# v projected with the tokens on the partitions, and placed by 16 DMAs a strip

## The chip, the core and the metric

The kernel runs on one core of one Trainium2 chip. Its time is the device time of one execution in microseconds (us). Engines: TensorE (PE in the profile), VectorE (DVE), ScalarE (ACT), GpSimd (POOL), SyncE (SP); PEld is the loading of weights, which overlaps PE. The data are float32 but for the gates.

## The reference

x is (8, 64, 96, 96). Two passes of window attention (4x4 windows, 8 heads of 4 channels, for each half of the channels) are made on the normalized x, the second on rows rolled by two; then a mixture of experts per pixel. Cut to what matters:

```python
qkv = einsum('oi,bihw->bohw', qkv_w, xh)            # xh: 32 channels of layernorm(x)
q, k, v = split(qkv, 3, axis=1)
lepe = depthwise_conv3x3(v, lepe_w)
attn = softmax(einsum('nhqc,nhkc->nhqk', q*scale, k) + bias)   # n: window, 16 tokens
out = einsum('nhqk,nhkc->nhqc', attn, v) + lepe
x = x + pass(shift 0) + pass(shift 2)
t = tokens(x); y = layernorm(t)
t = t + sum over the top 2 of 8 experts of gate * (y @ expert_w[e] + expert_b[e])
```

## The kernel before

The image is worked in strips of 4 rows (384 pixels, 24 windows): 24 strips an image, 192 in all. On the partitions lie 4 groups of 32 channels: both halves of the channels of both passes, so one strip serves both. A strip is three units of 8 windows. The whole program is a software pipeline of slots, one unit a slot, three a strip, six a tile (two strips of the experts' part). Every engine walks the same slots in order, and in each slot does the stages whose turn it is; `LAG` gives for each stage how many slots it comes after a strip's (or unit's) first. There is no scheduler: an engine's instructions run in program order, and semaphores join the engines. A stage of strip k at lag L stands in slot 3k+L; a stage that is done for each unit stands in slots 3k+L to 3k+L+2.

The stages around the change:

- `centre` (lag 0) and `variance` (1): TensorE centres the strip, ScalarE makes the reciprocal deviation, and VectorE multiplies (L989), which signals `xn_made`.
- `value` (2): TensorE multiplies the strip by `wv` (L570, for attention) and `wo` (L572, for the convolution); ScalarE evicts the first twice, once for each value of a mask, into `v2` (L697), and the second into the padded image `vpad` (L701).
- `query_key` (3), `spread_k` (4): q and k; GpSimd spreads k by 4 DMAs (L476).
- `turn_v` (5): VectorE transposes `v2` to `v2t` in 32x32 blocks (L939).
- `tap_products` (6), `pool_taps` (7), `taps` (10): nine taps of the convolution. ScalarE makes three products, one a slot (L744); GpSimd adds the second and third to the first (L493), in the slots 3k+8 and 3k+9; VectorE does the other six, two a slot (L906), and the first of them waits for both of GpSimd's additions (L902). ScalarE's second and third product of a strip wait for GpSimd's addition of the strip before (L742).
- `spread_v` (7): GpSimd places `v2t` into `vx`, the weights of the product, by 4 DMAs (L484). It waits for `v2t_made`, and, `vx` having two buffers, for the products of strip k-2 (L481).
- `score` (7), `shift` (8), `turn_p` (10), `product` (11): scores by 32x32 tiles (L541), softmax without its division, transposed probabilities (L981), 32 small matmuls with `vx` as weights (L607), and in a strip's last unit the sums over `ones` (L612); then `pv_made` rises by one.
- `experts` (35): TensorE spreads a gate (L516), VectorE multiplies (L895), TensorE applies the expert (L525), eight times a tile; before the change the first expert of a slot comes ahead of `value`.

```python
wait_alone(pool, v2t_made, k + 1)
if s.later(r, 2):
    wait_alone(pool, pv_made, (k - 1) * UNITS)
```

Of the kernel before, what the change touches and what calls it, by code (L numbers as in the profile page):

```python
# [32 lines left out]
ALU = mybir.AluOpType  # L33
# [6 lines left out]
SP = 4  # L40
# [26 lines left out]
    spread_k=4, turn_v=5, place_bias=6, spread_v=7, score=7, shift=8,  # L67
# [80 lines left out]
def _constants():  # L148
    p = np.arange(128)
    g, c = p // CH, p % CH  # L150
    same64 = (p[:, None] // C == p[None, :] // C).astype(np.float32)
    parts = {
        "ident": np.eye(128),
        "centre": np.eye(128) - same64 / C,
        "mean": same64 / C,

        "mask_q": ((p[:, None] // 16 & 1) == np.arange(2)[None, :]) * HD ** -0.5,
        "mask_v": (p[:, None] & 1) == np.arange(2)[None, :],
        "ones": (p[:, None] // 32 == np.arange(32)[None, :] // 8) & (p[:, None] // TOK % 2 == np.arange(32)[None, :] % 2),
        "mask_b": (p[:, None] // TOK % 4) == p[None, :4],  # L160

        "expert_sel": np.stack([(p[:, None] % E == e) & (p[:, None] // E % 2 == p[None, :] // C)
                                & (p[:, None] < 3 * GE) for e in range(E)], axis=1).reshape(128, E * 128),
        "rank": np.tile(E - np.arange(E), (128, 1)),
        "eps1": np.full((128, 1), LN1_EPS),
        "eps2": np.full((128, 1), LN2_EPS),
    }
# [10 lines left out]
def metaformer_block(nc, x, qkv_w, lepe_w, bias_table, router_w, router_b, expert_w, expert_b, consts, out):  # L178
    ctx = ExitStack()
    with ctx:  # L180
# [43 lines left out]
        v2 = sb("v2", [128, 2, WIN, 2, TOK])  # L224
        v2t = sb("v2t", [128, 2, 8, WIN, 4])
        qx = sb("qx", [128, 2, WIN, 2, TOK])
        kx = sb("kx", [128, 2, 4, SPX])
        vx = sb("vx", [128, 2, 32, WIN * 4])
# [38 lines left out]
        v2_made, v2t_made = sem("v2_made"), sem("v2t_made")  # L267
# [49 lines left out]
        X_DMAS, Z_DMAS, TILE_DMAS, K_DMAS, V_DMAS = 5, 11, 7, 4, 4  # L317
# [4 lines left out]
        def _(sp):  # L322
# [134 lines left out]
        def _(pool):  # L457
# [7 lines left out]
            G.memset(vx[:, :, :, :].rearrange("p a c n -> p (a c n)"), 0.0).then_inc(spread_cleared, 1)  # L465
# [3 lines left out]
            def slot(s):  # L469
# [29 lines left out]
        def _(pe):  # L499
# [9 lines left out]
            def slot(s):  # L509
# [20 lines left out]
                if u := s.unit("score"):  # L530
# [34 lines left out]
                if st := s.strip("value"):  # L565
                    k, r = st
                    pe.wait_ge(xn_made, k + 1)
                    if ti := s.tile("router"):
                        pe.wait_ge(fln_made, ti[0] + 1)
                    MM(bank_p[0][:, 0:SPX], wv[:, :], xs[:, r % 4, :], start=True, stop=True).then_inc(v_made, 1)  # L570
                    pe.wait_ge(ln_made, k + 1)
                    MM(bank_p[1][:, 0:SPX], wo[:, :], xs[:, r % 4, :], start=True, stop=True).then_inc(vo_made, 1)  # L572
                if st := s.strip("query_key"):
# [4 lines left out]
                    MM(bank_p[1][:, 0:SPX], wk[:, :], xs[:, r % 4, :], start=True, stop=True).then_inc(k_made, 1)  # L578
                if st := s.strip("query_key"):
                    k, r = st  # L580
                    pe.wait_ge(v2_made, (k + 1) * 2)
                    MM(bank_p[0][:, 0:SPX], wq[:, :], xs[:, r % 4, :], start=True, stop=True).then_inc(q_made, 1)  # L582
# [10 lines left out]
                if u := s.unit("product"):  # L593
# [10 lines left out]
                    for w in range(UW):  # L604
                        at = (j * UW + w)
                        for c in range(4):
                            last = MM(bank_o[32 * c:32 * c + 32, at * TOK:(at + 1) * TOK],  # L607
                                      vx[:, kr % 2, :, at * 4 + c],
# [45 lines left out]
        def _(act):  # L654
# [12 lines left out]
            def slot(s):  # L667
# [23 lines left out]
                if st := s.strip("value"):  # L691
                    k, r = st
                    act.wait_ge(v_made, k + 1)
                    if s.later(r, 2):
                        act.wait_ge(v2t_made, k - 1)
                    for x in range(2):
                        S.activation(v2[:, r % 2, :, x, :].rearrange("p n (r w) -> p n r w", w=SP),  # L697
                                     windows(bank_p[0][:, 0:SPX]), ACT.Copy,
                                     scale=const("mask_v")[:, x:x + 1]).then_inc(v2_made, 1)
                    act.wait_ge(vo_made, k + 1)  # L700
                    S.activation(vrows(r, 0, 0), bank_p[1][:, 0:SPX].rearrange("p (r w) -> p r w", w=W),  # L701
# [12 lines left out]
                if st := s.strip("query_key"):  # L714
# [4 lines left out]
                    for a in range(2):  # L719
                        S.activation(qx[:, r % 2, :, a, :].rearrange("p n (r w) -> p n r w", w=SP),  # L720
                                     windows(bank_p[0][:, 0:SPX]), ACT.Copy,
                                     scale=const("mask_q")[:, a:a + 1]).then_inc(q_saved, 1)
                if st := s.strip("query_key"):
# [5 lines left out]
                    S.activation(by_window(k_sb[:, r % 2, :]), windows(bank_p[1][:, 0:SPX]),  # L729
# [35 lines left out]
        def _(dve):  # L765
# [13 lines left out]
            for g in range(4):  # L779
# [3 lines left out]
                for b in range(2):  # L783
                    some = heads_of(2, g).rearrange("p (h a b y) -> p b h a y", h=HD, a=2, b=2)[:, b]
                    V.tensor_copy(wv[:, g * CH + 16 * b:g * CH + 16 * b + 16].rearrange("p (a h y) -> p h a y", a=2, y=2), some)
# [89 lines left out]
            def slot(s):  # L875
# [58 lines left out]
                if st := s.strip("turn_v"):  # L934
                    k, r = st
                    dve.wait_ge(v2_made, (k + 1) * 2)
                    if s.later(r, 2):
                        dve.wait_ge(v_spread[r % 2], k // 2 * (V_DMAS * 16))
                    V.transpose(v2t[:, r % 2, :, :, :].rearrange("p q n k -> p n k q"), v2[:, r % 2, :, :, :].rearrange("p n x i -> p (n x i)")).then_inc(v2t_made, 1)  # L939
# [76 lines left out]
```

## Time and profile before

| | |
|---|---|
| median of 3 runs | 4068.01 us (4063.95 to 4075.65) |
| profiled execution | 4055.97 us, span 4054.1 us |
| mean granted TensorE clock | 0.967 of full speed |
| PE, DVE, ACT, POOL busy | 92%, 79%, 57%, 30% of the span |
| chain that ended last | PE 72%, DVE 12%, issue 7%, ACT 7% |
| DMA engines busy (mean of 16) | about 25% of the span |

The span is from the first to the last instruction. A busy share says how long an engine was at work, not whether anyone waited for it; the chain follows back from the last instruction to what released each step, so it says where time would be won or lost. A wait is put down to the instruction that ended it. DMAs issued by GpSimd take time on GpSimd for each of them, and that time counts as its busy time.

### The profile page before, as it was taken

What the parts mean: (1) busy time and instruction counts of PE and PEld (TensorE: products, weight loads), DVE (VectorE), ACT (ScalarE), POOL (GpSimd) and SP (SyncE); (2) the same over time, 40 slices, a digit from 0 to 9 for tenths busy, and PEclk for the clock granted to TensorE, in tenths of its full rate; (3) what the DMA queues carried; (4) which work ended last, traced back from release to release, by engine and by line L of the source; (5) the groups of instructions that cost most, each with busy time, mean ns of one, the idle gap of its engine ahead of it and who ended that gap; (6) DMA issues with size and microseconds to landing.
All of it is one profiled execution on the core that took longest, in us unless ns stands there. A gap on an engine that the chain in (4) does not pass through costs nothing.

```text
span 4054.1 us, 199188 instructions
## 1 busy us (share of the span) xinstructions
PE 3712.7 (92%) x81317; PEld 2244.7 (55%) x81317; DVE 3193.6 (79%) x7043; ACT 2299.6 (57%) x4708; POOL 1207.9 (30%) x1930
## 2 busy tenths in 40 slices
PE   3999999998999989999999989999899999999987
PEld 2655555555555555555555555555555555555552
DVE  3888888887887878787788878788788888888773
ACT  3755665655665555655555555556565656566540
POOL 2433333322333323333232323333233333333320
PEclk9999999999999999999999999999999999999985
DMA  2222222222222222222222222222222222222220
GB/s 41 79 66 75 70 76 68 78 69 68 70 74 69 74 65 75 68 75 68 68 71 68 72 66 73 68 75 69 73 69 73 70 75 67 75 69 76 67 56 22
DMA packets 191590, 278.78 MB, mean 69 GB/s; under 512 B 67584, under 2 KB 153648, under 8 KB 190640
## 3 DMA queue, kind: packets, MB, share of 16 engines
q1 hardware_dynamic: 141488, 152.22, 14.0%
q0 software_dynamic: 49152, 113.34, 9.8%
q8 instruction: 663, 10.86, 1.1%
q14 instruction: 287, 2.35, 0.2%
HBM read 95.46 MB, written 56.62 MB: 38 GB/s over the span
## 4 chain that ended last, share of the span: by engine, by line
PE 72%; DVE 12%; issue 7%; ACT 7%; SPq 1%; DVEq 1%; DMA 0%; ACTq 0%
PE bank L607 20%; PE bank L525 13%; PE bank L541 10%; DVE v2t L939 5%; PE bank L578 4%; PE bank L564 4%; PE bank L620 4%; PE bank L516 3%; PE bank L612 3%; PE bank L582 3%; DVE gx L895 3%; ACT row_inv L679 2%; PE bank L634 2%; ACT row_inv L677 2%; PE bank L639 1%
## 5 line engine op out<-in xcount | busy, mean ns | idle before, releaser
L607 PEld LDWEIGHTS bank<-probT,vx 128*32 128x32 f32 x36864 | 831.3, 193 | 201.8 <-issue 171.4
L607 PE MATMUL bank<-probT,vx 128*32 128x16 f32 x36864 | 888.4, 236 | 3.0 <-issue 2.2
L525 PE MATMUL bank<-gx,expert_sb 128*128 128x384 f32 x1536 | 714.0, 548 | 190.8 <-DVE gx L895 190.8
L895 DVE TENSOR_TENSOR gx<-bank,yn 128x384 f32<-128x384 f32 x768 | 423.6, 552 | 557.0 <-PE bank L516 554.9
L476 POOL DMA_DIRECT2D kx<-k_sb x768 | 411.3, 538 | 1194.9 <-ACT k_sb L729 1108.3
L541 PEld LDWEIGHTS bank<-kx,qx 32*32 32x32 f32 x36864 | 565.6, 108 | 302.5 <-issue 299.7
L541 PE MATMUL bank<-kx,qx 32*32 32x64 f32 x36864 | 664.3, 221 | 40.9 <-issue 31.6
L484 POOL DMA_DIRECT2D vx<-v2t x768 | 380.7, 503 | 911.0 <-PE bank L612 857.8
L493 POOL TENSOR_TENSOR lepe_p<-lepe_p,tap_sb 128x384 f32<-128x384 f32 x384 | 406.4, 1058 | 604.7 <-ACT tap_sb L744 601.2
L906 DVE SCALAR_TENSOR_TENSOR lepe<-vpad,lepe_sb,lepe 128x384 f32<-128x384 f32 x960 | 582.1, 606 | 0.0
L706 ACT ACTIVATE prob<-prob 128x512 f32<-128x512 f32 x576 | 363.1, 630 | 230.1 <-DVE prob L926 229.9
L525 PEld LDWEIGHTS bank<-gx,expert_sb 128*128 128x128 f32 x1536 | 243.5, 194 | 416.4 <-DVE gx L895 356.3
L981 DVE STREAM_TRANSPOSE probT<-prob 128x512 f32<-128x512 f32 x576 | 404.1, 702 | 0.0
L926 DVE TENSOR_TENSOR prob<-bank,row_max 128x512 f32<-128x512 f32 x576 | 393.1, 682 | 11.9 <-issue 7.8
L914 DVE TENSOR_REDUCE row_max<-bank 128x32 f32<-128x512 f32 x576 | 393.2, 683 | 11.7 <-issue 9.5
L697 ACT ACTIVATE v<-bank,const_sb 128x384 f32<-128x384 f32 x384 | 201.8, 577 | 334.2 <-PE bank L570 334.2
L720 ACT ACTIVATE qx<-bank,const_sb 128x384 f32<-128x384 f32 x384 | 205.3, 587 | 316.1 <-PE bank L582 316.1
L712 ACT ACTIVATE bank<-bias_tile 128x512 f32<-128x512 f32 x576 | 341.8, 593 | 0.0
L939 DVE STREAM_TRANSPOSE v2t<-v 128x768 f32<-128x768 f32 x192 | 291.7, 1519 | 0.2
L516 PEld LDWEIGHTS bank<-gateT,expert_sel 48*128 48x128 bf16 x768 | 71.6, 93 | 389.0 <-issue 382.6
L516 PE MATMUL bank<-gateT,expert_sel 48*128 48x384 bf16 x768 | 260.0, 338 | 0.0
L734 ACT ACTIVATE xs<-bank 128x384 f32<-128x384 f32 x192 | 94.1, 490 | 264.1 <-PE bank L620 264.1
(100 smaller groups left out, 4701.3 us busy)
## 6 DMA issues: line engine op xcount, KB each, us to landing
vx<-v2t POOLq DMA_DIRECT2D x768, 96.0 KB, 2.7
kx<-k_sb POOLq DMA_DIRECT2D x768, 48.0 KB
z<-fin SPq DMA_DIRECT2D x1344, 24.0 KB
xs<-in_x SPq DMA_DIRECT2D x96, 192.0 KB
xt<-in_x SPq DMA_DIRECT2D x192, 96.0 KB
z0t<-z SPq DMA_DIRECT2D x192, 96.0 KB
out_y<-y_out SPq DMA_DIRECT2D x192, 96.0 KB, 2.7
xs<-in_x SPq DMA_DIRECT2D x96, 139.5 KB
```

The costliest lines, as they stand in the source:

```text
L476: pool.dma_start(kx[m:128:4, r % 2, m, :], k_sb[m:128:4, r % 2, :]).then_inc(k_spread[r % 2], 16)
L493: G.tensor_tensor(lepe_p[:, kr % 2, :], lepe_p[:, kr % 2, :], tap_sb[:, j - 1, :], ALU.add).then_inc(pool_lepe_made, 1)
L516: MM(bank_g[:, 0:SPX], expert_sel[:, e, :], gateT[:, r % 2, :], start=True, stop=True)\
L525: MM(bank_f[:, 0:SPX], expert_sb[:, e, :], gx[:, e % 2, :], start=False, stop=(e == E - 1))\
L541: last = MM(bank_s[r % 2][at, w * KEYS:(w + 1) * KEYS], qx[at, kr % 2, win, :, :].rearrange("p a i -> p (a i)"), kx[at, kr % 2, :, win * T ...
L607: last = MM(bank_o[32 * c:32 * c + 32, at * TOK:(at + 1) * TOK], vx[:, kr % 2, :, at * 4 + c], probT[:, kr % 2, at, c * TOK:(c + 1) * TOK] ...
L895: V.tensor_tensor(gx[:, e % 2, :], bank_g[:, 0:SPX], yn[:, r % 2, :], ALU.mult).then_inc(gx_made, 1)
L906: V.scalar_tensor_tensor(acc, vrows(r, t // 3 - 1, t % 3 - 1), lepe_sb[:, t:t + 1], first if j == 0 else acc, ALU.mult, ALU.add).then_inc( ...
L914: V.tensor_reduce(row_max[:, r % 2, :], per_row(bank_s[r % 2][:, :]), AX.X, ALU.max).then_inc(max_made, 1)
L926: V.tensor_tensor(per_row(prob[:, r % 4, :]), per_row(bank_s[r % 2][:, :]), over_keys(row_max[:, r % 2, :]), ALU.subtract).then_inc(shifte ...
L939: V.transpose(v2t[:, r % 2, :, :, :].rearrange("p q n k -> p n k q"), v2[:, r % 2, :, :, :].rearrange("p n x i -> p (n x i)")).then_inc(v2 ...
L981: V.transpose(probT[:, kr % 2, j * UW:(j + 1) * UW, :].rearrange("p n k -> p (n k)"), prob[:, r % 4, :]).then_inc(probT_made, 1)
```

## The change

v for the attention is made with the tokens, not the channels, on the partitions. VectorE's multiply writes the normalized strip into a new buffer `xw` in the order of windows, and all four projections read it. Each pair of windows has 32 tokens; for each pair and each group of 32 channels one matmul with the 32x32 block of `xw` as weights and the block of `wv` as moving data gives 32 tokens by 32 channels, 48 matmuls a strip. ScalarE evicts them once, into `vt`. VectorE's transpose and `turn_v` are gone. GpSimd places `vt` into `vx` by 16 DMAs of 16 partitions in place of 4 of 32, as a token of an odd window has to move to another partition. `spread_v` has lag 5 in place of 7. The value matmuls stand right behind the scores, ahead of the first expert. The eviction of v waits for the DMAs of strip k-2, and the loads of x wait for `xn_made` in place of `q_made`.

```diff
-    spread_k=4, turn_v=5, place_bias=6, spread_v=7, score=7, shift=8,
+    spread_k=4, place_bias=6, spread_v=5, score=7, shift=8,
...
-        X_DMAS, Z_DMAS, TILE_DMAS, K_DMAS, V_DMAS = 5, 11, 7, 4, 4
+        X_DMAS, Z_DMAS, TILE_DMAS, K_DMAS, V_DMAS = 5, 11, 7, 4, 16
...
-                        wait_alone(sp, q_made, (k - 1) * 2)
+                        wait_alone(sp, xn_made, (k - 1) * 2)
...
                 if st := s.strip("spread_v"):
                     k, r = st
-                    wait_alone(pool, v2t_made, k + 1)
+                    wait_alone(pool, vt_saved, k + 1)
                     if s.later(r, 2):
                         wait_alone(pool, pv_made, (k - 1) * UNITS)
                     for g in range(4):
-                        rows = slice(32 * g, 32 * g + 32)
-                        pool.dma_start(vx[rows, r % 2, g * 8:g * 8 + 8, :].rearrange("p q n -> p (q n)"),
-                                     v2t[rows, r % 2, :, :, :].rearrange("p q n k -> p (q n k)")).then_inc(v_spread[r % 2], 16)
+                        for x in range(2):
+                            for odd in range(2):
+                                to, at = g * CH + x * TOK, g * CH + odd * TOK
+                                pool.dma_start(vx[to:to + TOK, r % 2, g * 8 + x:g * 8 + 8:2, odd, :],
+                                               vt[at:at + TOK, r % 2, x::2, :, :].rearrange("p h n k -> p h (n k)"))\
+                                    .then_inc(v_spread[r % 2], 16)
...
+                if st := s.strip("value"):
+                    k, r = st
+                    if ti := s.tile("router"):
+                        pe.wait_ge(fln_made, ti[0] + 1)
+                    wait_alone(pe, xn_made, k + 1)
+                    for pair in range(WIN // 2):
+                        cols = slice(pair * CH, pair * CH + CH)
+                        for g in range(4):
+                            at = slice(g * CH, g * CH + CH)
+                            last = MM(bank_p[0][at, cols], xw[at, r % 2, cols], wv[at, at], start=True, stop=True)
+                    last.then_inc(v_made, 1)
...
-                    MM(bank_p[0][:, 0:SPX], wv[:, :], xs[:, r % 4, :], start=True, stop=True).then_inc(v_made, 1)
                     pe.wait_ge(ln_made, k + 1)
-                    MM(bank_p[1][:, 0:SPX], wo[:, :], xs[:, r % 4, :], start=True, stop=True).then_inc(vo_made, 1)
+                    MM(bank_p[1][:, 0:SPX], wo[:, :], xw[:, r % 2, :], start=True, stop=True).then_inc(vo_made, 1)
...
                     if s.later(r, 2):
-                        act.wait_ge(v2t_made, k - 1)
-                    for x in range(2):
-                        S.activation(v2[:, r % 2, :, x, :].rearrange("p n (r w) -> p n r w", w=SP),
-                                     windows(bank_p[0][:, 0:SPX]), ACT.Copy,
-                                     scale=const("mask_v")[:, x:x + 1]).then_inc(v2_made, 1)
+                        act.wait_ge(v_spread[r % 2], k // 2 * (V_DMAS * 16))
+                    S.activation(vt[:, r % 2, :, :, :].rearrange("p q n k -> p n q k"),
+                                 bank_p[0][:, 0:SPX].rearrange("p (n q k) -> p n q k", q=8, k=4),
+                                 ACT.Copy).then_inc(vt_saved, 1)
...
-                    V.transpose(v2t[:, r % 2, :, :, :].rearrange("p q n k -> p n k q"), v2[:, r % 2, :, :, :].rearrange("p n x i -> p (n x i)")).then_inc(v2t_made, 1)
...
-                    V.tensor_tensor(xs[:, r % 4, :], xs[:, r % 4, :], rstd[:, r % 2, :], ALU.mult).then_inc(xn_made, 1)
+                    if s.later(r, 2):
+                        dve.wait_ge(q_made, k - 1)
+                    V.tensor_tensor(by_window(xw[:, r % 2, :]), windows(xs[:, r % 4, :]), windows(rstd[:, r % 2, :]),
+                                    ALU.mult).then_inc(xn_made, 1)
```

GpSimd's queue at the start of the pipeline, before: k's DMAs go into `kx`, v's into `vx`, and the additions on `lepe_p` are those of the convolution, two a strip.

```order
L476 DMA kx<-k_sb 32x384 [waits k_saved,const_loaded,spread_cleared]
L476 DMA kx<-k_sb 32x384 x3
L476 DMA kx<-k_sb 32x384 [waits k_saved]
L476 DMA kx<-k_sb 32x384 x3
L484 DMA vx<-v2t 32x768 [waits v2t_made]
L484 DMA vx<-v2t 32x768 x3
L493 ISA
L493 TENSOR_TENSOR lepe_p<-lepe_p,tap_sb 128x384 [waits tap_made]
L493 TENSOR_TENSOR lepe_p<-lepe_p,tap_sb 128x384 [waits pool_lepe_made,tap_made]
```

The same place after the change:

```order
L475 DMA kx<-k_sb 32x384 [waits k_saved,const_loaded,spread_cleared]
L475 DMA kx<-k_sb 32x384 x3
L485 DMA vx<-vt 16x4x48 [waits vt_saved]
L485 DMA vx<-vt 16x4x48 x15
L475 DMA kx<-k_sb 32x384 [waits k_saved]
L475 DMA kx<-k_sb 32x384 x3
L485 DMA vx<-vt 16x4x48 [waits vt_saved]
L485 DMA vx<-vt 16x4x48 x15
L495 ISA
L495 TENSOR_TENSOR lepe_p<-lepe_p,tap_sb 128x384 [waits tap_made]
L495 TENSOR_TENSOR lepe_p<-lepe_p,tap_sb 128x384 [waits pool_lepe_made,tap_made]
```

Before, v of strip 0 stands ahead of strip 0's additions; after, v of strips 0 and 1 does, and so on: v of strip k comes right ahead of the additions of strip k-1. From the third strip on v's first DMA also waits for `pv_made`, in both.

TensorE from one strip's last product to the next strip's first, before, where no experts are at work yet:

```order
L612 MATMUL bank<-probT,const_sb 32x384 x4
L541 MATMUL bank<-kx,qx 32x64 [waits bias_placed]
L541 MATMUL bank<-kx,qx 32x64 x31
L570 MATMUL bank<-xs,wv 128x384 [waits xn_made]
L572 MATMUL bank<-xs,wo 128x384 [waits ln_made]
L607 MATMUL bank<-probT,vx 32x16 [waits picked,log_made,v_spread1,probT_made]
L607 MATMUL bank<-probT,vx 32x16 x31
```

And after the change:

```order
L621 MATMUL bank<-probT,const_sb 32x384 x4
L543 MATMUL bank<-kx,qx 32x64 [waits bias_placed]
L543 MATMUL bank<-kx,qx 32x64 x31
L557 MATMUL bank<-wv,xw 32x32 [waits xn_made]
L557 MATMUL bank<-wv,xw 32x32 x47
L581 MATMUL bank<-xw,wo 128x384 [waits ln_made]
L616 MATMUL bank<-probT,vx 32x16 [waits picked,log_made,v_spread1,probT_made]
L616 MATMUL bank<-probT,vx 32x16 x31
```

One matmul over the whole strip is now 48 small ones, with the same wait ahead of them.

## Rows read from the trace of the kernel before

**Rows 1.** The page: busy us (share) and instructions, and the chain that ended last.
```profile
PE 3712.7 (92%) x81317; PEld 2244.7 (55%) x81317; DVE 3193.6 (79%) x7043; ACT 2299.6 (57%) x4708; POOL 1207.9 (30%) x1930
...
PE 72%; DVE 12%; issue 7%; ACT 7%; SPq 1%; DVEq 1%; DMA 0%; ACTq 0%
PE bank L607 20%; PE bank L525 13%; PE bank L541 10%; DVE v2t L939 5%; PE bank L578 4%; PE bank L564 4%; PE bank L620 4%; PE bank L516 3%; PE bank L612 3%; PE bank L582 3%; DVE gx L895 3%; ACT row_inv L679 2%; PE bank L634 2%; ACT row_inv L677 2%; PE bank L639 1%
```

**Rows 2.** Groups of instructions: count | busy us, mean ns | idle before, releasers.
```profile
L476 POOL DMA_DIRECT2D kx<-k_sb x768 | 411.3, 538 | 1194.9 <-ACT k_sb L729 1108.3 <-issue 59.1 <-PE bank L541 27.4
...
L484 POOL DMA_DIRECT2D vx<-v2t x768 | 380.7, 503 | 911.0 <-PE bank L612 857.8 <-issue 52.2
L939 DVE STREAM_TRANSPOSE v2t<-v 128x768 f32<-128x768 f32 x192 | 291.7, 1519 | 0.2
...
L966 DVE TENSOR_TENSOR fin<-att,lepe 128x384 f32<-128x384 f32 x192 | 105.6, 550 | 0.0
```

**Rows 3.** Line 484 alone: ns min/median/max, first and last start in us.
```profile
L484 POOL DMA_DIRECT2D vx<-v2t x768: 496/504/513, 70.8 to 3915.5; - x192
...
DMA to landing us min/median/max: 2.1/2.7/6.9
```

**Rows 4.** Waits of GpSimd: us in total, times, longest.
```profile
POOL vx L484 <- PE bank L612: 857.8, 183, 11.9
```

**Rows 5.** Timeline from 2000 us, TensorE and GpSimd: start, us, instruction [idle before].
```profile
2000.99 0.86 PE L612 MATMUL bank<-probT,const_sb 128*32 128x384 f32 x7
...
2002.50 1.98 POOL L484 DMA_DIRECT2D vx<-v2t  x4 [3.67 <-PE bank L612]
...
2003.38 1.10 PE L541 MATMUL bank<-kx,qx 32*32 32x64 f32 x64
...
2004.41 0.91 PE L525 MATMUL bank<-gx,expert_sb 128*128 128x384 f32 x2
...
2005.52 0.91 PE L570 MATMUL bank<-xs,wv 128*128 128x384 f32 x2
...
2006.26 0.81 PE L572 MATMUL bank<-xs,wo 128*128 128x384 f32 x2
...
2015.69 1.48 PE L607 MATMUL bank<-probT,vx 128*32 128x16 f32 x64
```

**Rows 6.** The same stretch, VectorE.
```profile
2001.50 0.68 DVE L914 TENSOR_REDUCE row_max<-bank 128x32 f32<-128x512 f32 x1
...
2003.58 0.56 DVE L895 TENSOR_TENSOR gx<-bank,yn 128x384 f32<-128x384 f32 x1 [1.40 <-PE bank L516]
...
2020.66 0.61 DVE L906 SCALAR_TENSOR_TENSOR lepe<-vpad,lepe_sb,lepe_p 128x384 f32<-128x384 f32 x1
...
2022.53 0.55 DVE L989 TENSOR_TENSOR xs<-xs,rstd 128x384 f32<-128x384 f32 x1
```

**Rows 7.** Timeline from 3894 us, all engines.
```profile
3896.48 0.84 PE L612 MATMUL bank<-probT,const_sb 128*32 128x384 f32 x7
...
3898.28 0.91 PE L525 MATMUL bank<-gx,expert_sb 128*128 128x384 f32 x2
...
3899.96 2.15 POOL L493 TENSOR_TENSOR lepe_p<-lepe_p,tap_sb 128x384 f32<-128x384 f32 x2
...
3902.70 1.65 PE L525 MATMUL bank<-gx,expert_sb 128*128 128x384 f32 x2 [3.24 <-DVE gx L895]
...
3904.28 1.53 PE L607 MATMUL bank<-probT,vx 128*32 128x16 f32 x64
```

**Rows 8.** Timeline of TensorE alone, a little later.
```profile
3905.74 1.93 PE L541 MATMUL bank<-kx,qx 32*32 32x64 f32 x64
```

**Rows 9.** Windows: length, busy (instructions) of PE, PEld, DVE, ACT, POOL, clock, DMA share, GB/s.
```profile
88.00:92.00 4.00, 3.52 (x67) 2.63 (x68) 3.96 (x6) 1.10 (x3) 1.00 (x1) 0.60 0.02 6
92.00:96.00 4.00, 3.70 (x132) 2.79 (x131) 3.55 (x7) 3.80 (x8) 1.13 (x1) 0.97 0.02 4
...
3960.00:3965.00 5.00, 3.70 (x6) 1.20 (x6) 2.34 (x9) 0.00 (x0) 0.00 (x0) 0.50 0.20 51
```

More of the change, by code:

```diff
@@ L157, in _constants @@
         "mask_q": ((p[:, None] // 16 & 1) == np.arange(2)[None, :]) * HD ** -0.5,
-        "mask_v": (p[:, None] & 1) == np.arange(2)[None, :],
         "ones": (p[:, None] // 32 == np.arange(32)[None, :] // 8) & (p[:, None] // TOK % 2 == np.arange(32)[None, :] % 2),
@@ L223, in metaformer_block @@
         k_sb = sb("k_sb", [128, 2, SPX])
-        v2 = sb("v2", [128, 2, WIN, 2, TOK])
-        v2t = sb("v2t", [128, 2, 8, WIN, 4])
+        xw = sb("xw", [128, 2, SPX])
+        vt = sb("vt", [128, 2, 8, WIN // 2, 4])
         qx = sb("qx", [128, 2, WIN, 2, TOK])
         kx = sb("kx", [128, 2, 4, SPX])
-        vx = sb("vx", [128, 2, 32, WIN * 4])
+        vx = sb("vx", [128, 2, 32, 2, WIN // 2 * 4])
         prob = sb("prob", [128, 4, UK])
@@ L266, in metaformer_block @@
         q_made, k_made, q_saved, k_saved = sem("q_made"), sem("k_made"), sem("q_saved"), sem("k_saved")
-        v2_made, v2t_made = sem("v2_made"), sem("v2t_made")
+        vt_saved = sem("vt_saved")
         k_spread, v_spread, spread_cleared = sems("k_spread"), sems("v_spread"), sem("spread_cleared")
@@ L464, in _ @@
             G.memset(kx[:, :, :, :].rearrange("p a c n -> p (a c n)"), 0.0).then_inc(spread_cleared, 1)
-            G.memset(vx[:, :, :, :].rearrange("p a c n -> p (a c n)"), 0.0).then_inc(spread_cleared, 1)
+            G.memset(vx[:, :, :, :, :].rearrange("p a c b n -> p (a c b n)"), 0.0).then_inc(spread_cleared, 1)
             pool.wait_ge(const_loaded, 16 * N_WEIGHT_DMAS)
@@ L566, in slot @@
                     k, r = st
-                    pe.wait_ge(xn_made, k + 1)
-                    if ti := s.tile("router"):
-                        pe.wait_ge(fln_made, ti[0] + 1)
-                    MM(bank_p[0][:, 0:SPX], wv[:, :], xs[:, r % 4, :], start=True, stop=True).then_inc(v_made, 1)
                     pe.wait_ge(ln_made, k + 1)
-                    MM(bank_p[1][:, 0:SPX], wo[:, :], xs[:, r % 4, :], start=True, stop=True).then_inc(vo_made, 1)
+                    MM(bank_p[1][:, 0:SPX], wo[:, :], xw[:, r % 2, :], start=True, stop=True).then_inc(vo_made, 1)
                 if st := s.strip("query_key"):
@@ L577, in slot @@
                     pe.wait_ge(v_saved, k + 1)
-                    MM(bank_p[1][:, 0:SPX], wk[:, :], xs[:, r % 4, :], start=True, stop=True).then_inc(k_made, 1)
+                    MM(bank_p[1][:, 0:SPX], wk[:, :], xw[:, r % 2, :], start=True, stop=True).then_inc(k_made, 1)
                 if st := s.strip("query_key"):
                     k, r = st
-                    pe.wait_ge(v2_made, (k + 1) * 2)
-                    MM(bank_p[0][:, 0:SPX], wq[:, :], xs[:, r % 4, :], start=True, stop=True).then_inc(q_made, 1)
+                    pe.wait_ge(vt_saved, k + 1)
+                    MM(bank_p[0][:, 0:SPX], wq[:, :], xw[:, r % 2, :], start=True, stop=True).then_inc(q_made, 1)
                 expert(1)
@@ L607, in slot @@
                             last = MM(bank_o[32 * c:32 * c + 32, at * TOK:(at + 1) * TOK],
-                                      vx[:, kr % 2, :, at * 4 + c],
+                                      vx[:, kr % 2, :, at % 2, at // 2 * 4 + c],
                                       probT[:, kr % 2, at, c * TOK:(c + 1) * TOK], start=True, stop=True)
@@ L719, in slot @@
                     for a in range(2):
-                        S.activation(qx[:, r % 2, :, a, :].rearrange("p n (r w) -> p n r w", w=SP),
-                                     windows(bank_p[0][:, 0:SPX]), ACT.Copy,
+                        S.activation(qx[:, r % 2, :, a, :], bank_p[0][:, 0:SPX].rearrange("p (n i) -> p n i", i=TOK), ACT.Copy,
                                      scale=const("mask_q")[:, a:a + 1]).then_inc(q_saved, 1)
@@ L728, in slot @@
                         act.wait_ge(k_spread[r % 2], k // 2 * (K_DMAS * 16))
-                    S.activation(by_window(k_sb[:, r % 2, :]), windows(bank_p[1][:, 0:SPX]),
+                    S.activation(k_sb[:, r % 2, :], bank_p[1][:, 0:SPX],
                                  ACT.Copy).then_inc(k_saved, 1)
@@ L784, in _ @@
                     some = heads_of(2, g).rearrange("p (h a b y) -> p b h a y", h=HD, a=2, b=2)[:, b]
-                    V.tensor_copy(wv[:, g * CH + 16 * b:g * CH + 16 * b + 16].rearrange("p (a h y) -> p h a y", a=2, y=2), some)
+                    V.tensor_copy(wv[:, g * CH:(g + 1) * CH].rearrange("p (h y b a) -> p b h a y", h=HD, y=2, b=2)[:, b], some)
                     last = V.tensor_copy(wo[:, 64 * b:64 * b + 64].rearrange("p (a g h y) -> p g h a y", a=2, g=4, y=2)[:, g], some)
@@ L933, in slot @@
                 gate_work((0, 0), (0, 0), (13, 14))
[L934 to L938, printed above, removed]
-                    V.transpose(v2t[:, r % 2, :, :, :].rearrange("p q n k -> p n k q"), v2[:, r % 2, :, :, :].rearrange("p n x i -> p (n x i)")).then_inc(v2t_made, 1)
                 if yt := s.tile("tile_sum"):
```

2 lines of the change are left out of this document (1 added, 1 removed).

## The prediction

> **What bounds the kernel now.** I read first the busy shares and the chain of work that ended last. TensorE is busy 92% of the span and holds 72% of the chain; VectorE 79% and 12%; GpSimd is busy 30% and holds no part of the chain [rows 1]. The reader is to see that TensorE sets the pace, that VectorE is close behind it, and that GpSimd looks free. The chain's line on the transposes of v, 5%, is the only large piece of it that this change takes out. Then the groups of instructions give durations [rows 2], the first and last start of the placing DMAs give the pace of a strip, (3915.5 - 70.8) / 191 = 20.1 us [rows 3], and the waits of GpSimd say what its queue hangs on: 183 of the 192 times it comes to v's DMAs it waits for line 612, the last matmuls of a product [rows 4]. That wait costs nothing now, since whatever stands behind it on GpSimd is wanted much later. The timeline of a strip then gives distances in time between the engines [rows 5, 6].
>
> **The wait that is moved.** A slot is a third of a strip. For strip k, GpSimd's place for v's DMAs goes from slot 3k+7 to slot 3k+5. But the wait in front of them is unchanged: `pv_made` must reach (k-1)*3, which is the last product of strip k-2, and TensorE does that at slot 3(k-2)+2+11 = 3k+7. So GpSimd stands at its place for 3k+5 until TensorE has finished the product of 3k+7. Behind it in the queue are now the two tap additions of strip k-1 (slots 3k+5 and 3k+6); before, the ones behind it were those of strip k (slots 3k+8 and 3k+9). The order rows of GpSimd show this at the start: two strips' v ahead of the first tap, where one strip's stood. And the first tap of VectorE for strip k-1, at slot 3k+7, waits for both additions. It stands ahead of `turn_p` and of the multiply that makes `xn_made`, for which TensorE's value matmuls at slot 3k+8 wait. ScalarE's second tap product at slot 3k+7 waits for the first of those additions too. So every strip has a closed loop: product ends, 16 DMA issues, two additions, VectorE's rest of a slot, value matmuls, and on to the next strip's product. It can't be run ahead of, as each step is in program order.
>
> **Its length.** Let t0 be the end of the last product, 2000.99 + 0.86 = 2001.85 in the timeline. I count to the start of the first expert matmul at the next slot.
> - t0 to the first issue on GpSimd: 2002.50 - 2001.85 = 0.65 us [rows 5].
> - 16 issues. Four take 1.98 now, 0.495 each [rows 5]. The new ones have 16 partitions of 4 runs of 192 bytes, 64 runs, where the old had 32. If the price is per instruction, 16 x 0.495 = 7.9; if it is per run, twice 0.503 [rows 2], 16.1. No row shows 64 runs. The nearest row with another shape is k's: 32 runs of half the bytes at 0.538 [rows 2], so a shape costs a little and bytes don't. I take 0.60 each, 9.6 us.
> - two additions back to back: 2.15 [rows 7].
> - VectorE from that tap to the end of the multiply: 2022.53 + 0.55 - 2020.66 = 2.42 [rows 6].
> - 48 small matmuls. The 32 of a score unit, of the same 32x32 tiles, take 2004.41 - 2003.38 = 1.03 [rows 5], so 1.55; their 32 moving columns are half of the score's 64, so the lower end is 0.8, and the upper, at the half clock below, 2.8. Meanwhile VectorE makes the row maximum and gx (0.68 + 0.56, [rows 6]), which fits beside them.
>
> Sum 0.65 + 9.6 + 2.15 + 2.42 + 1.55 = 16.4 us. Before, the same distance was 2004.41 - 2001.85 = 2.56 in one strip [rows 5] and 3898.28 - 3897.32 = 0.96 in a strip of the other kind [rows 7]: mean 1.8. Added per strip: 14.6.
>
> **What it gives back.** The old value matmul goes from its later place: 2006.26 - 2005.52 = 0.74 [rows 5]. The transposes (192 x 1.519 us [rows 2]) leave VectorE; on the path they were 5% of 4054 us, 1.06 a strip [rows 1], and I credit all of it. One of v's two evictions leaves ScalarE, and the evictions read other patterns; ScalarE is 57% busy and 7% of the chain [rows 1], and in the new stall it waits too: nothing, and at most 0.4 either way if that cover goes. The multiply writes in window order: VectorE's add for `fin` is windowed on both sides and takes 0.550, no more than the plain multiply's 0.55 [rows 2, 6]: nothing, at most 0.1 either way. Placing k comes behind the additions, and its DMAs are wanted two slots later: nothing. The new wait of the eviction of v on the DMAs of strip k-2 ends about 2.7 us [rows 3] after the last issue, at t0 + 13, before the value matmuls end at t0 + 16.4: nothing, unless a landing takes over 6 us (the longest took 6.9). SyncE waits for an earlier signal than before: nothing. Left: 14.6 - 0.74 - 1.06 = 12.8.
>
> **The clock.** In the stall TensorE has only a score (1.1 us) and at times some tile work left, so of the 14.8 us to the end of the multiply it stands about 12. After an idle of 3.24 us before the expert matmul at 3902.70 the two matmuls take 1.65 where they took 0.91 at 3898.28 [rows 7]; that is 1.2 instead of 2.4 GHz, a factor of 1.8. The score at 3905.74 is still slow, 1.93 for 1.10 [rows 5, 8]. In the start of the run the granted clock was 0.60 in the 4 us in which TensorE was busy 3.52, and 0.97 in the next [rows 9]. I take a spell of 5 us at the low level after each stall, which does the work of 5/1.8: 2.2 us lost. Bounds: 1 and, if it never comes back, the rival below.
>
> The Trainium skill, "TensorE: Matmul & The Clock Gate", section on HAM oscillation, says that gaps in which the array waits let the clock fall back in every tile of a loop, so the cost is paid each time; by that rule this term is there in every strip, and the trace agrees at the one such gap in its steady part. Without the rule, at no clock loss, the sum would be 190 x 2.2 = 420 us less.
>
> **The sum.** 12.8 + 2.2 = 15.0 us a strip. The wait stands in all strips but the first two: 190 x 15.0 = 2850. On the profiled execution's 4056 us (span 4054) that is 6906; the median of the runs shown is 12 us above the profiled one, so I say 6910 us.
>
> The Trainium skill, "DMA: Bandwidth & Descriptors", section "Anatomy of one DMA — SWDGE (gpsimd) path", says that many descriptors can be generated before their cost shows. By that rule the issues would be at the 7.9 end and the time about 6590. The same page's rules for kernel authors ask for small transfers to be merged, which speaks against 16 of them. No row here shows either for this shape.
>
> **Rivals.**
> - An issue is priced by its runs: 16.1 instead of 9.6, 6.5 more a strip, 6906 + 190 x 6.5 = 8140 us. For it: nothing but the doubled count. Against: bytes and stride hardly move the price between the two rows there are. 16 in 100.
> - The clock does not come back within the strip. For it: in the tail of the run it stays at 0.50 while TensorE is busy 3.70 of 5 us [rows 9]. Against: there VectorE gates each expert; in the steady part the work is dense. Of the strip's 20.1 us about 14 are matmuls that the clock stretches: 92% busy, less line 607's 20% [rows 1], since a product took 1.53 right after that idle for 1.48 otherwise [rows 5, 7]: 11 more, of which it fills about 1 of VectorE waits and replaces the 2.2: +8, 8400 us. 11 in 100.
> - The stall isn't there, because something lets GpSimd pass early, and TensorE pays for the small matmuls only: 192 x (1.55 - 0.74) = 156, 4210 us. For it: GpSimd is idle 70% of the time. Against: the wait's count and the order of the queue. 6 in 100.
> - The other side: again no stall, as the DMAs are issued where GpSimd is idle, and VectorE's 1.06 of the chain outweighs the 0.81 of TensorE: 192 x -0.25 = -48, 4010 us. It decides only if taps don't wait for v's DMAs. 4 in 100.
> - My forecast, with its own range of 6150 (issues at 7.9, clock 1, matmuls 0.8) to 7600: 63 in 100.
>
> **The numbers.** 6910 us, range 6150 to 8300, which leaves out the last two rivals and about half of the clock's. Within 0.3% (about what a measurement of this kernel can tell from no change) only by chance between the last two: 1 in 100, slower 95, faster 4.
>
> **What would show it.** In the profile after: v's DMAs in one block of 16 after each last product, with the two additions right behind and VectorE's first tap waiting for the second of them; a wait of VectorE for GpSimd of about 10 us, 190 times; TensorE's value matmuls waiting for the multiply; the granted clock near 0.8 and matmul durations in two groups; TensorE's busy share near 60%. Wrong if VectorE's tap has no wait for GpSimd, if a strip's pace is under 30 us, or if GpSimd's block is longer than 12 us.

## The result and the profile after

The changed kernel takes 6591.2 us (median of 4 runs, 6568.82 to 6598.91) against 4065.98 before: 1.621 times as long, 95% interval 1.614 to 1.628. The forecast was 6910 us, with a range of 6150 to 8300.

The page of the profiled execution: busy shares, the chain that ended last by engine and by line, and three of the costliest groups (as in [rows 1, 2]).

```profile
span 6591.1 us, 237016 instructions
...
PE 4140.8 (63%) x99365; PEld 2534.9 (38%) x99365; DVE 2875.1 (44%) x6851; ACT 2216.5 (34%) x4516; POOL 2341.3 (36%) x4234
...
PE 57%; POOL 28%; issue 8%; DVE 4%; ACT 1%; SPq 1%; DVEq 1%; POOLq 0%; DMA 0%; ACTq 0%
POOL vx L485 22%; PE bank L616 13%; PE bank L527 12%; PE bank L543 6%; POOL lepe_p L495 6%; PE bank L557 4%; PE bank L581 4%; PE bank L518 3%; PE bank L587 3%; PE bank L577 3%; PE bank L629 2%; PE bank L621 2%; PE bank L591 2%; DVE xw L992 2%; DVE lepe L913 1%
...
L485 POOL DMA_DIRECT2D vx<-vt x3072 | 1554.3, 515 | 4028.2 <-PE bank L621 3940.6
L557 PE MATMUL bank<-wv,xw 32*32 32x32 f32 x18432 | 290.1, 236 | 2272.9 <-DVE xw L992 2271.4
L913 DVE SCALAR_TENSOR_TENSOR lepe<-vpad,lepe_sb,lepe_p 128x384 f32<-128x384 f32 x192 | 119.3, 622 | 2891.5 <-POOL lepe_p L495 2891.5
```

GpSimd held nothing of the chain in [rows 1]; now it holds 28%, and 22% are the issues of v's DMAs and 6% the two additions, though its own busy share rose only from 30% to 36%. An engine idle 64% of the time holds the others up, since it is idle at the wrong time. Every other engine's share fell: they wait.

The waits of the whole span (us in total, times, longest); [rows 4] had 857.8 us for v's DMAs:

```profile
POOL vx L485 <- PE bank L621: 3940.6, 190, 29.2
DVE lepe L913 <- POOL lepe_p L495: 2891.5, 191, 19.2
...
PE bank L557 <- DVE xw L992: 2271.4, 190, 16.0
ACT tap_sb L751 <- POOL lepe_p L495: 2039.7, 190, 15.0
```

Each wait of the loop stands here, 190 or 191 times: v's DMAs for the product, the tap for the additions, the value matmuls for the multiply; what lies between them is queue order. ScalarE's second tap product waits for the first addition as well. And one strip of it in the timeline (start, us, instruction, count, idle before):

```profile
3009.80 0.82 PE L621 MATMUL bank<-probT,const_sb 128*32 128x384 f32 x7
...
3011.32 8.09 POOL L485 DMA_DIRECT2D vx<-vt  x16 [19.22 <-PE bank L621]
...
3019.42 2.08 POOL L495 TENSOR_TENSOR lepe_p<-lepe_p,tap_sb 128x384 f32<-128x384 f32 x2
...
3021.53 0.62 DVE L913 SCALAR_TENSOR_TENSOR lepe<-vpad,lepe_sb,lepe_p 128x384 f32<-128x384 f32 x1 [15.11 <-POOL lepe_p L495]
...
3023.19 0.55 DVE L992 TENSOR_TENSOR xw<-xs,rstd 128x384 f32<-128x384 f32 x1
...
3023.84 1.50 PE L557 MATMUL bank<-wv,xw 32*32 32x32 f32 x96 [10.61 <-DVE xw L992]
...
3025.28 1.65 PE L527 MATMUL bank<-gx,expert_sb 128*128 128x384 f32 x2
```

It answers to [rows 5, 6]: from the end of the last product, t0 = 3009.80 + 0.82 = 3010.62 to the first expert at 3025.28 are 14.66 us, where 2.56 stood. The next strip has 14.96.

### The profile page after: what moved, and what is told of

Same layout as the page of the kernel before. It is cut to its first block, busy times and chain, and to the rows that moved or that the text cites. A ratio compares the mean times of both kernels' runs of the same rounds, so it can differ in the third digit from the quotient of the medians.

```text
span 6591.1 us, 237016 instructions
## 1 busy us (share of the span) xinstructions
PE 4140.8 (63%) x99365; PEld 2534.9 (38%) x99365; DVE 2875.1 (44%) x6851; ACT 2216.5 (34%) x4516; POOL 2341.3 (36%) x4234
## 4 chain that ended last, share of the span: by engine, by line
PE 57%; POOL 28%; issue 8%; DVE 4%; ACT 1%; SPq 1%; DVEq 1%; POOLq 0%; DMA 0%; ACTq 0%
POOL vx L485 22%; PE bank L616 13%; PE bank L527 12%; PE bank L543 6%; POOL lepe_p L495 6%; PE bank L557 4%; PE bank L581 4%; PE bank L518 3%; PE bank L587 3%; PE bank L577 3%; PE bank L629 2%; PE bank L621 2%; PE bank L591 2%; DVE xw L992 2%; DVE lepe L913 1%
## 5 line engine op out<-in xcount | busy, mean ns | idle before, releaser
L485 POOL DMA_DIRECT2D vx<-vt x3072 | 1554.3, 515 | 4028.2 <-PE bank L621 3940.6
L557 PE MATMUL bank<-wv,xw 32*32 32x32 f32 x18432 | 290.1, 236 | 2272.9 <-DVE xw L992 2271.4
L913 DVE SCALAR_TENSOR_TENSOR lepe<-vpad,lepe_sb,lepe_p 128x384 f32<-128x384 f32 x192 | 119.3, 622 | 2891.5 <-POOL lepe_p L495 2891.5
L557 PEld LDWEIGHTS bank<-wv,xw 32*32 32x32 f32 x18432 | 269.6, 150 | 2300.1 <-issue 2299.8
L527 PE MATMUL bank<-gx,expert_sb 128*128 128x384 f32 x1536 | 906.6, 681 | 50.2 <-DVE gx L902 50.2
L751 ACT ACTIVATE tap_sb<-vpad,lepe_sb 128x384 f32<-128x384 f32 x384 | 237.9, 619 | 2039.7 <-POOL lepe_p L495 2039.7
L543 PE MATMUL bank<-kx,qx 32*32 32x64 f32 x36864 | 643.7, 218 | 26.3 <-issue 16.5
L527 PEld LDWEIGHTS bank<-gx,expert_sb 128*128 128x128 f32 x1536 | 334.9, 250 | 262.2 <-DVE gx L902 162.2
L495 POOL TENSOR_TENSOR lepe_p<-lepe_p,tap_sb 128x384 f32<-128x384 f32 x384 | 383.4, 999 | 31.6 <-ACT tap_sb L751 10.6
L705 ACT ACTIVATE vt<-bank 128x384 f32<-128x384 f32 x192 | 94.2, 491 | 610.0 <-PE bank L557 610.0
```

Of the source, the lines that this page charges most:

```text
L485: pool.dma_start(vx[to:to + TOK, r % 2, g * 8 + x:g * 8 + 8:2, odd, :], vt[at:at + TOK, r % 2, x::2, :, :].rearrange("p h n k -> p h (n k)"))\
L495: G.tensor_tensor(lepe_p[:, kr % 2, :], lepe_p[:, kr % 2, :], tap_sb[:, j - 1, :], ALU.add).then_inc(pool_lepe_made, 1)
L527: MM(bank_f[:, 0:SPX], expert_sb[:, e, :], gx[:, e % 2, :], start=False, stop=(e == E - 1))\
L543: last = MM(bank_s[r % 2][at, w * KEYS:(w + 1) * KEYS], qx[at, kr % 2, win, :, :].rearrange("p a i -> p (a i)"), kx[at, kr % 2, :, win * T ...
L557: last = MM(bank_p[0][at, cols], xw[at, r % 2, cols], wv[at, at], start=True, stop=True)
L913: V.scalar_tensor_tensor(acc, vrows(r, t // 3 - 1, t % 3 - 1), lepe_sb[:, t:t + 1], first if j == 0 else acc, ALU.mult, ALU.add).then_inc( ...
```

## The experiments

Eleven kernels ran; the ratios are to the kernel before, run again beside each group of them.

**Where v's DMAs stand.** The first takes the changed kernel and gives v's DMAs their old lag back.

```diff
-    spread_k=4, place_bias=6, spread_v=5, score=7, shift=8,
+    spread_k=4, place_bias=6, spread_v=7, score=7, shift=8,
```

> The changed kernel with v's DMAs at lag 7, their place before the change. Theory (queue order makes the loop): the taps no longer stand behind v's DMAs, so VectorE's wait of 15 us for GpSimd goes. But v's eviction at slot 3k+8 waits for the DMAs of strip k (two buffers), which start only after the product of 3k+7: landed about 11 us after t0, where ScalarE wants to evict at t0+4.6. The next score's bias comes about 4.3 us late, with 1 us of clock: near 5000 us, with ScalarE waiting for v's DMAs. Rival (the lag alone is the fault and nothing else): 4010 to 4210 us.

5273.7 us (1.301, 1.296 to 1.307). The 2892 us of VectorE's wait for GpSimd are gone, and the predicted second loop stands in the waits:

```profile
ACT vt L705 <- DMA vx<-vt: 1637.1, 190, 11.8
```

It cost more than I reckoned, 6.4 us a strip and not 5.3. The eviction waits 8.6 us in the mean, and 9.22 in the strip that I read, in which GpSimd paused 2.18 us between v's eighth and ninth DMA (such pauses are 87.7 us in this run, 0.46 a strip). TensorE stands 5.45 us there behind the padded v, after which a score takes 1.93: the clock had fallen again. So the lag alone does not mend it; with two buffers, DMAs issued late hold the eviction instead of the taps.

The second takes that wait away by more buffers.

```diff
-        vt = sb("vt", [128, 2, 8, WIN // 2, 4])
+        vt = sb("vt", [128, 4, 8, WIN // 2, 4])
...
-                    if s.later(r, 2):
-                        act.wait_ge(v_spread[r % 2], k // 2 * (V_DMAS * 16))
+                    if s.later(r, 4):
+                        act.wait_ge(v_spread[r % 4], k // 4 * (V_DMAS * 16))
```

> The same with four buffers of vt (and four semaphores), so that the eviction waits for the DMAs of strip k-4. Theory: no loop is left, 16 DMAs and 48 small matmuls cost only TensorE's 0.8 us and VectorE's transposes give up to 1.06 us: 4010 to 4210 us, clock back near 0.97. Rival (the many small DMAs or matmuls cost in themselves, by the clock, the ports or GpSimd's time): 4400 us and more.

4145.2 us (1.024, 1.021 to 1.027), clock 0.962. Both loops are gone, and with them 2446 of the 2525 us. What is left is the change itself: 95 us over the kernel before as it ran beside this one.

The third leaves v as it was and moves only its 4 DMAs in the kernel before.

```diff
-    spread_k=4, turn_v=5, place_bias=6, spread_v=7, score=7, shift=8,
+    spread_k=4, turn_v=5, place_bias=6, spread_v=5, score=7, shift=8,
```

> The kernel before with only v's 4 DMAs moved from lag 7 to lag 5. Theory: the same loop with 2.0 us of issues in place of 8.1. First expert at t0 + 0.65 + 2.0 + 2.1 + 2.2 + 1.24 = 8.2 in place of 1.8, so 6.4 us a strip and about 2 of clock: near 5650 us, VectorE's first tap waiting for GpSimd's addition. Rival (the 16 DMAs and the small matmuls are the cause, the place is harmless): 4060 us.

5456.6 us (1.347, 1.341 to 1.352). One number in a table makes the kernel before 35% slower. Its strip:

```profile
2999.67 0.84 PE L612 MATMUL bank<-probT,const_sb 128*32 128x384 f32 x8
3001.18 1.99 POOL L484 DMA_DIRECT2D vx<-v2t  x4 [22.68 <-PE bank L612]
3003.18 2.07 POOL L493 TENSOR_TENSOR lepe_p<-lepe_p,tap_sb 128x384 f32<-128x384 f32 x2
...
3005.36 0.62 DVE L906 SCALAR_TENSOR_TENSOR lepe<-vpad,lepe_sb,lepe_p 128x384 f32<-128x384 f32 x1 [8.27 <-POOL lepe_p L493]
...
3009.04 1.65 PE L525 MATMUL bank<-gx,expert_sb 128*128 128x384 f32 x2 [7.50 <-DVE gx L895]
```

From t0 = 3000.51 to the expert are 8.53 us, 8.2 forecast; the total is 3% under the forecast, as I had put the clock at about 2 us a strip here too.

The last of this group leaves the lag at 5 and takes away what v's DMAs wait for, by a third buffer of `vx`.

```diff
-                    if s.later(r, 2):
-                        wait_alone(pool, pv_made, (k - 1) * UNITS)
+                    if s.later(r, 3):
+                        wait_alone(pool, pv_made, (k - 2) * UNITS)
```

> The changed kernel at lag 5 as it is, with three buffers of vx in place of two, so that v's DMAs wait for the products of strip k-3, which end at slot 3k+4. Theory (the place at lag 5 costs only through that wait): no wait of VectorE for GpSimd, 4110 to 4200 us like the run at lag 7 with four buffers of vt. Rival (place or number of DMAs in front of the additions is harmful in itself): 4400 us and more.

4127.1 us (1.020, 1.016 to 1.025), and VectorE's tap waits for GpSimd 5 times, 11.7 us in all. GpSimd itself still waits at this place:

```profile
POOL vx L485 <- PE bank L621: 949.9, 188, 6.6
```

But it waits for the product of one strip earlier, and what stands behind it is then in time. So the same place in the queue, with a wait at its head, costs nothing of the loop. This settles the cause: neither the lag nor the 16 DMAs by themselves, but a wait that ends two slots after its place, with work behind it that other engines need by then.

**What the number of DMAs costs.** Only even windows and half of the heads are placed, three quarters of v are left out.

```diff
-        X_DMAS, Z_DMAS, TILE_DMAS, K_DMAS, V_DMAS = 5, 11, 7, 4, 16
+        X_DMAS, Z_DMAS, TILE_DMAS, K_DMAS, V_DMAS = 5, 11, 7, 4, 4
...
-                        for x in range(2):
-                            for odd in range(2):
+                        for x in range(1):
+                            for odd in range(1):
```

> The changed kernel with 4 of the 16 DMAs (x = 0, even windows only), so that three quarters of v are not placed. Theory: the issues stand in the loop one for one: 12 x 0.505 = 6.1 us less a strip, 6590 - 190 x 6.1 = 5430 us, some 100 less if the clock's loss shrinks with the idle. Rival (the loop is set by something else, such as the landing or the matmuls): above 6000 us.

5371.8 us (1.326). 1219 us less than 6591 for 12 x 190 DMAs, 0.535 each, against 0.515 for one issue: one for one, and the little above it goes with the clock (0.833 for 0.779). In the loop an issue is worth its full time.

**What the low clock costs.** Matmuls of 128 columns that serve nothing fill TensorE's stall. The first try stood behind the wait for `fln_made` in half of the strips and was too short in the others.

```diff
+                    if s.later(r, 2):
+                        for _ in range(30):
+                            MM(bank_p[0][:, SPX:512], const("centre"), const_sb[:, 0:128], start=True, stop=True)
```

> The changed kernel with 30 matmuls of 128 columns into an unused part of a bank, ahead of TensorE's wait for the multiply (from the third strip on), so that it works in most of the stall. The loop itself is the same. Theory (clock term 2.2 to 2.8 us a strip): granted clock back above 0.93, 190 x 2.2 to 2.8 less, 6060 to 6170 us. Rival (the low clock costs nothing, as the loop's other steps set the pace): within 50 us of 6590; if the filling takes longer than the stall, more.

7010.2 us: it tells nothing of the clock's price. In the strips with tile work the filling began only when the wait ended, at the stall's end, and lengthened the loop (TensorE waited 816 us at its head); in the others it ran 6.96 us, left 5.6 idle, and the expert after it still took 1.65.

The second stands ahead of both waits, with 46 or 40 matmuls, in the bank of the experts' sum, whose value it spoils.

```diff
+                    if s.later(r, 2):
+                        for _ in range(46 if s.tile("router") is None else 40):
+                            MM(bank_f[:, SPX:512], const("centre"), const_sb[:, 0:128], start=True, stop=True, skip_group_check=True)
```

> The changed kernel with the filling made right: it stands ahead of both waits of the value stage, in a bank that nobody reads in the stall, and is 46 matmuls (40 in strips with tile work) at 0.232 us each, 10.7 and 9.3 us of a stall of 12 and 10.5. Theory (half clock after each stall costs 2.2 to 2.8 us a strip, and nothing else changes): granted clock above 0.95, first expert after the stall 0.91 and not 1.65, 6060 to 6170 us. Rival (the clock's loss lies beside waits that stay): above 6400.

6418.4 us (1.584), granted clock 0.944 for 0.779. It gives back 173 us, 0.91 a strip. That misses the forecast of 420 to 530 and falls to the rival, above 6400. The filling held the clock in a part of the strips. Two strips with 40 matmuls: in the first GpSimd paused 2.18 us in its block, 3.71 us stayed idle, and the expert took 1.65 again; in the second, without a pause, 1.55 stayed idle, and it took 0.91. With 46 matmuls and 2.99 us left idle it took 1.65 too.

```profile
2996.30 9.20 PE L552 MATMUL bank<-const_sb 128*128 128x128 f32 x80
3009.20 1.51 PE L560 MATMUL bank<-wv,xw 32*32 32x32 f32 x96 [3.71 <-DVE xw L995]
3010.64 1.65 PE L527 MATMUL bank<-gx,expert_sb 128*128 128x384 f32 x2
...
3064.91 9.20 PE L552 MATMUL bank<-const_sb 128*128 128x128 f32 x80
3075.65 1.01 PE L560 MATMUL bank<-wv,xw 32*32 32x32 f32 x96 [1.55 <-issue]
3076.67 0.91 PE L527 MATMUL bank<-gx,expert_sb 128*128 128x384 f32 x2
```

Three quarters of what the clock lacks to full speed came back (0.165 of 0.22), so the whole is some 1.2 us a strip by proportion, an estimate; I had said 2.2 and, before this run, up to 2.8.

**What is left of the change without the loop.** The 48 value matmuls stand in the profile as 96 matmuls (PE) and 96 weight loads (PEld), those of a score as 64 and 64. In the run at 4145 us TensorE stands idle inside the former, at nothing that the profile shows, 1.67 us in this strip:

```profile
2004.49 0.96 PE L557 MATMUL bank<-wv,xw 32*32 32x32 f32 x89
...
2007.12 0.26 PE L557 MATMUL bank<-wv,xw 32*32 32x32 f32 x7 [1.67 <-issue]
```

The waits of this run have it twice, as the weight loads stand still together with the matmuls:

```profile
PEld bank L557 <- issue: 108.5, 94, 3.0
...
PE bank L557 <- issue: 92.9, 90, 2.6
PE bank L565 <- DVE gate_part L879: 92.9, 67, 3.0
```

So TensorE loses 93 us here; the 201 us in the expectations below are the sum of both lines, which counts each pause twice. The last line is a second wait that grew: TensorE turns the gates (L565) behind VectorE's arithmetic on them, and waited 5.9 us for it in the kernel before.

Four kernels ask why, all on the version at lag 7 with four buffers of vt. With 4 of the 16 DMAs (three quarters of v not placed):

```diff
-        X_DMAS, Z_DMAS, TILE_DMAS, K_DMAS, V_DMAS = 5, 11, 7, 4, 16
+        X_DMAS, Z_DMAS, TILE_DMAS, K_DMAS, V_DMAS = 5, 11, 7, 4, 4
...
-                        for x in range(2):
-                            for odd in range(2):
+                        for x in range(1):
+                            for odd in range(1):
```

> Lag 7 and four buffers of vt, with 4 of the 16 DMAs (three quarters of v not placed). In the run with all 16, TensorE stood 201 us inside the small value matmuls at nothing the profile shows. Theory A (the DMAs of 192 bytes, issued in the same moment, hold up TensorE's instruction fetch): the idle at this line falls to a third, time 4040 to 4080 us. Theory B (the run of 192 short instructions outruns the fetch by itself): it stays, 4110 to 4150 us.

4041.4 us (0.9965, 0.9945 to 0.9984), but the idle inside the value matmuls stays:

```profile
PE bank L557 <- issue: 96.4, 90, 2.6
...
PE bank L565 <- DVE gate_part L879: 8.1, 5, 3.0
```

The time fits theory A and the mechanism refutes it: the 104 us came from elsewhere, 85 of them from TensorE's wait for the gates, which VectorE now has ready. The groups of VectorE show why it was late, first with 16 DMAs, then with 4:

```profile
L967 DVE TENSOR_TENSOR fin<-att,lepe 128x384 f32<-128x384 f32 x192 | 169.9, 885 | 0.0
```

```profile
L967 DVE TENSOR_TENSOR fin<-att,lepe 128x384 f32<-128x384 f32 x192 | 127.0, 662 | 0.0
```

550 ns stood in [rows 2]. VectorE's busy time is 3120 us with 16 DMAs and 2954 with 4. After 16 DMAs GpSimd's two additions come back to back and meet VectorE's work; after 4 they stand some 5 us apart (2012.44 and 2017.41 in that run). With 16:

```profile
2012.39 1.13 DVE L861 TENSOR_SCALAR gate_vec<-gate_vec 128x6 f32<-128x6 f32 x1
2012.47 2.08 POOL L495 TENSOR_TENSOR lepe_p<-lepe_p,tap_sb 128x384 f32<-128x384 f32 x2
...
2013.80 1.18 DVE L946 TENSOR_TENSOR y<-xt,z0t 128x384 f32<-128x384 f32 x1
```

The first of these takes 0.16 and the last 0.55 elsewhere. The Trainium skill, "SBUF — State Buffer", section "Who interferes with whom", says that a VectorE instruction with two inputs in SBUF and a GpSimd instruction that reads SBUF share a read port, and that one waits for the other whole. The trace agrees with 1.18 for 0.55, while VectorE's reads of PSUM (`gx` 0.555, the row maximum 0.684) are what they were. The first row, 1.13 for 0.16, has one tensor as its input, and that sentence doesn't cover it.

With the value matmuls back behind the first expert and the variance (the block of 11 lines is taken from the head of TensorE's slot and stands behind them):

```diff
-                if st := s.strip("value"):
-                    k, r = st
-                    if ti := s.tile("router"):
-                        pe.wait_ge(fln_made, ti[0] + 1)
-                    wait_alone(pe, xn_made, k + 1)
...
+                    if ti := s.tile("router"):
+                        pe.wait_ge(fln_made, ti[0] + 1)
+                    wait_alone(pe, xn_made, k + 1)
...
```

> Lag 7 and four buffers, with the value matmuls back behind the first expert and the variance, where the one matmul stood. If the idle inside them comes from following straight on the 128 instructions of a score (theory B), it shrinks and the time is 4070 to 4110 us; if it comes from the DMAs (theory A), nothing or little changes: 4120 to 4160 us.

3957.6 us (0.977, 0.974 to 0.980): faster than both kernels. TensorE's idle inside falls from 92.9 us (90 times) to 20.5 (34 times), so it goes with 192 short instructions standing right behind the 128 of a score (theory B). That is 72 of the 188 us. The wait for the gates is 71.9 now, 21 less, and TensorE's busy time 3709 for 3776, at a granted clock of 0.977 for 0.962. Why the clock rose no run shows; VectorE waits less for the spread gate (590 us for 784), since the first expert no longer stands behind the value matmuls. I had expected 4070 to 4110 and thought of the first part alone.

With v's DMAs held back a slot, behind the value matmuls of strip k+2:

```diff
-    spread_k=4, place_bias=6, spread_v=7, score=7, shift=8,
+    spread_k=4, place_bias=6, spread_v=8, score=7, shift=8,
...
-                    wait_alone(pool, vt_saved, k + 1)
+                    wait_alone(pool, v_made, strips_to(s, k + 3))
```

> Lag 7 and four buffers, with v's DMAs held back to a slot later (lag 8) and behind the value matmuls of strip k+2, so that the two no longer coincide. Theory A: the idle inside the value matmuls goes, 4040 to 4090 us, unless it moves to the next run of small matmuls. Theory B: as the run with all 16 at lag 7, 4130 to 4160 us.

4090.4 us (1.009, 1.007 to 1.012) with 91.9 us of idle inside: again a time at the edge of what fits theory A, while the idle refutes it. Where its 55 us come from is open. `fin` takes 573 ns in place of 885, but VectorE's busy time is 3114 us as before (3120): its meetings with GpSimd only moved to other instructions. Both edits together, on the version with lag 7 and four buffers:

> Lag 7, four buffers and the value matmuls behind the first expert (the version at 3958 us), with v's DMAs held back a slot as well. By itself the delay gave 55 us where the value matmuls came first. If that gain came from VectorE no longer meeting GpSimd's two additions back to back, it adds up: 3900 to 3940 us. If it came from the DMAs and the value matmuls no longer meeting, it is gone here: 3945 to 3975 us.

3911.9 us (0.965, 0.962 to 0.968), the best version, 3.5% faster than before. `fin` takes 565 ns in place of 778 in the version without the delay, VectorE's busy time is 2977 us for 3111, and TensorE waits 12.9 us for the gates and not 71.9. So these 46 us go with VectorE and GpSimd meeting less, as forecast; that the 55 us of the run before had the same source is not borne out. VectorE's tap waits 190 us for GpSimd again, 99 times: the queue's slack is used up.

## Why the prediction was right

**The wait that is moved** held as written, link by link and in 190 strips. Its proof is not the profile after alone, but that it comes by the lag alone in the kernel before (5457) and goes by a third buffer alone in the changed one (4127).

**The length of the loop**, forecast 16.37 us from t0 to the first expert, is 14.66 and 14.96 in the two strips read:
- first issue 0.70 (0.65 forecast), additions 2.08 (2.15), tap to the end of the multiply 2.21 and 2.43 (2.42): right.
- value matmuls 1.44 (1.55): near by luck. I had reckoned them at the full clock, where they take 1.01, and they ran at the lower level, 1.50 (both in the rows of the filled stall).
- 16 issues: 8.09, and I had 9.6. This is the term that was mis-sized: 64 runs of 192 bytes cost 0.515 each [rows 2: 0.503 for 32 runs], the lower end of my bounds. With 8.09 the sum would have been 6620. The Trainium skill's "DMA: Bandwidth & Descriptors", section "Anatomy of one DMA — SWDGE (gpsimd) path", says that many descriptors can be generated before their cost shows, and this run agrees for twice the runs. In 47 cases GpSimd also paused at nothing shown, 86.6 us in all, 2.19 in one block after the eighth DMA; what that is stays open.

**What it gives back, and the clock.** The pace of a strip is (6447.1 - 7.6 - 65.0) / 191 = 33.4 us by the block's first and last starts, 13.2 more than before; 15.0 was forecast. Of these about 15.3 - 1.8 = 13.5 lie before the first expert (14.8 and the mean pause of 0.46), so all that comes after nets to about -0.3, where I had -0.74 - 1.06 + 2.2 = +0.4. That the net was close is luck, as two terms were too large and of opposite sign: the filled stall puts the clock near 1.2, and 0.5 of that are the value matmuls, counted above. The stall's clock is there, and so is a long spell behind it. The windows (us, busy and count of PE, PEld, DVE, ACT and POOL, clock, DMA share, GB/s) from the first value matmul on:

```profile
3023.80:3032.00 8.20, 8.16 (x169) 4.70 (x170) 6.66 (x13) 2.60 (x5) 0.00 (x0) 0.53 0.02 8
3032.00:3045.90 13.90, 13.90 (x299) 8.03 (x295) 5.55 (x13) 6.54 (x13) 0.00 (x0) 1.00 0.13 33
```

About 8 us at the lower level and not 5, and still it costs only about 1.2. In this spell TensorE also runs a product, which hardly stretches (1.58, and 1.47 and 1.56 at the full clock of the same strip); what else covers the rest is not shown. Then the transposes gave back about 0.3 a strip by the remainder (0.3 - 0.74 + 0.7), and not 1.06. Both are worked out, not measured alone; the clock's share rests on one run that recovered three quarters.

**The rivals.** Issues priced by runs: no, by 515 ns. A clock that does not come back: no, 1.00 in the last 14 us of the strip. No stall: no. But its two prices can be read where there is none: the change without the loop is 95 us slower, between the 4010 and 4210 that I gave. Neither of them knew of the idle inside the value matmuls (93 us) or of VectorE held by GpSimd, and through it TensorE (87 us more than before).

## What to carry to other kernels

Before a step is moved forward in an in-order queue, find when the wait at its head ends, not when its own input is ready; and list what stands behind it, also for later or earlier strips, and who waits for that. A busy share of 30% says nothing of an engine whose queue others depend on. And where a larger loop hides it, measure an idea only after the loop is gone: this one is 62% slower as it came, and with two more buffers, its DMAs later and its matmuls in their old place 3.5% faster.

## What the runs showed of the hardware that I had not expected

- A run of 192 small instructions right behind 128 others leaves TensorE idle inside it, 92.9 us over 90 times, and 20.5 us over 34 times when two larger matmuls stand between. The number of v's DMAs (96.4 us with 4) and their time (91.9 us a slot later) don't matter to it. That it is the fetching of instructions, as the expectations have it, is a guess that no run tests.
- After an idle of 3.71 us TensorE ran at the lower level again, although the filling had kept it busy for 9.20 us just before it; after the same filling and an idle of 1.55 us it did not.
- VectorE's short instructions on SBUF wait for GpSimd's additions: a 128x48 product took 1189 ns on average in the version at 3958 us, 201 in the kernel before. It was not new: another (L844) took 454 ns there, and 202 in the changed kernel (L851), where VectorE stands still while GpSimd adds.
